# Self-attention softmax in a Trainium2 decoder layer: exp per head on ScalarE straight from the scores, causal mask on VectorE

## The reference

```python
q = (x @ wq).reshape(B, T, N_KV, N_REP, HEAD_DIM)
k = einsum('bkhl,ld->bkhd', (x @ wk_down).reshape(B, T, N_KV, D_LAT), wk_up)
v = einsum('bkhl,ld->bkhd', (x @ wv_down).reshape(B, T, N_KV, D_LAT), wv_up)
scores = einsum('bqhrd,bkhd->bhrqk', q, k) * HEAD_DIM ** -0.5
probs = softmax(where(causal, scores, min), axis=-1)
y = einsum('bhrqk,bkhd->bqhrd', probs, v).reshape(B, T, 1024) @ wo
...
x = x + self_attention(layernorm(x))
x = x + cross_attention_and_mlp(layernorm(x), ctx)
x = x + quantised_ffn(x)          # bitlinear, gelu, bitlinear
```

## Time and profile before

| | |
|---|---|
| median of 3 runs | 319.96 us (319.79 to 321.28) |
| the profiled execution, its own time | 321.1 us |
| its span, first to last instruction | 319.2 us |
| PE / PEld busy | 95% / 78% of the span |
| DVE busy | 86% |
| ACT busy | 60% |
| POOL busy | 51% |
| granted TensorE clock, mean | 0.984 of full |

### The profile page before, as it was taken

One profiled execution on the slowest core, in us unless ns is written; L12 is line 12 of the kernel. 1 busy time (PEld: TensorE's weight loads), 2 busy tenths in 40 slices (PEclk: granted clock), 3 DMA queues, 4 the chain that ended last, 5 costly groups with the idle time before them and its releaser, 6 DMA issues.

```text
span 319.2 us, 8883 instructions
## 1 busy us (share of the span) xinstructions
PE 302.6 (95%) x3185; PEld 248.8 (78%) x3198; DVE 273.2 (86%) x488; ACT 191.0 (60%) x369; POOL 161.5 (51%) x315
## 2 busy tenths in 40 slices
PE   8798999999999999999999999999999999998756
PEld 8476787879888887897788878887887888786534
DVE  2228996898989799999999999989999998999973
ACT  3164435436247759478966854497445965776852
POOL 7337006282933523671778266306660485077873
PEclk9899999999999999999999999999999999999978
DMA  7999000000000000000001010000000010000011
GB/s 200 340 368 330 6 3 0 2 2 0 4 2 2 3 0 2 3 0 2 2 3 34 3 35 2 2 0 4 16 18 2 2 37 2 0 3 33 3 34 66
DMA packets 11954, 12.54 MB, mean 39 GB/s; under 512 B 1668, under 2 KB 11144, under 8 KB 11912
## 3 DMA queue, kind: packets, MB, share of 16 engines
q1 hardware_dynamic: 10648, 11.40, 10.9%
q10 hardware_dynamic: 1264, 0.59, 0.7%
HBM read 9.89 MB, written 2.10 MB: 38 GB/s over the span
## 4 chain that ended last, share of the span: by engine, by line
PE 77%; issue 6%; DVE 6%; POOL 5%; ACT 5%; DVEq 0%; POOLq 0%; ACTq 0%
PE bank L1724 8%; PE bank L1871 7%; PE bank L1804 6%; PE bank L1894 6%; PE bank L1822 6%; PE bank L1903 5%; PE quad L1784 4%; PE bank L1885 4%; PE bank L1730 4%; PE quad L1861 3%; PE bank L1942 3%; PE bank L1757 3%; PE bank L1718 2%; PE bank L1923 2%; PE bank L1932 2%
## 5 line engine op out<-in xcount | busy, mean ns | idle before, releaser
L845 ACT ACTIVATE c_p<-bank 77x512 f32<-77x512 f32 x64 | 35.7, 591 | 26.4 <-PE bank L1871 26.2
L1871 PE MATMUL bank<-ident,c_s 128*77 128x128 f32 x256 | 34.8, 274 | 0.4 <-DVE f_o L1369 0.4
L564 POOL TENSOR_SCALAR f_s<-f_mv 128x1 f32<-128x1 f32 x16 | 3.5, 220 | 62.0 <-DVE f_s L1325 61.4
L821 ACT ACTIVATE a_p<-bank 128x512 f32<-128x512 f32 x48 | 27.3, 601 | 10.5 <-PE bank L1804 10.1
L1894 PE MATMUL bank<-c_y,xw_s 128*128 128x128 f32 x256 | 31.5, 276 | 0.8 <-DVE c_y L1303 0.8
L1871 PEld LDWEIGHTS bank<-ident,c_s 128*77 128x77 f32 x256 | 29.5, 148 | 3.1 <-issue 1.0
L1894 PEld LDWEIGHTS bank<-c_y,xw_s 128*128 128x128 f32 x256 | 30.1, 192 | 1.3 <-issue 0.9
L1903 PE MATMUL bank<-xw_s,c_h 128*128 128x256 f32 x128 | 30.5, 381 | 0.0
L1273 DVE TENSOR_REDUCE c_nm<-quad 128x16 f32<-128x1232 f32 x16 | 23.0, 1436 | 4.2 <-PE quad L1861 4.1
L1903 PEld LDWEIGHTS bank<-xw_s,c_h 128*128 128x128 f32 x128 | 23.3, 190 | 3.6 <-ACT c_h L854 0.5
L1284 DVE TENSOR_TENSOR c_s<-quad,c_nm 128x616 f32<-128x616 f32 x32 | 24.5, 792 | 1.3
(11 more groups left out here) (139 smaller groups left out, 769.8 us busy)
## 6 DMA issues: line engine op xcount, KB each, us to landing
out<-f_o SPq DMA_DIRECT2D x16, 128.0 KB, 1.7
xres<-in_x SPq DMA_DIRECT2D x1, 1536.0 KB, 10.0
c_p<-in_wqT SPq DMA_DIRECT2D x2, 512.0 KB, 6.9
c_p<-in_wo SPq DMA_DIRECT2D x1, 1024.0 KB, 9.6
f_h<-in_fw1T SPq DMA_DIRECT2D x1, 1024.0 KB, 12.1
c_s<-in_fw2T SPq DMA_DIRECT2D x1, 1024.0 KB, 11.3
xw_s<-in_xw SPq DMA_DIRECT2D x2, 512.0 KB, 9.7
fb_s<-in_fb SPq DMA_DIRECT2D x1, 512.0 KB, 6.3
```

The source lines that it names most:

```text
L821: nc.scalar.activation(dst, src, ACT.Exp, scale=SCALE_SA).then_inc(sa.sem["act"], 1)
L845: nc.scalar.activation(c_p[0:M, :, qt * P:(qt + 1) * P].rearrange("p (c j g) t -> p c j g t", c=KC, g=Q2)[:, :, j, :, :], bank("xs", f"tr{ ...
L1871: last = nc.tensor.transpose(dst[0:M, g * P:(g + 1) * P], c_s[:, qt, j, g, :], ident[:, :])
```

## The change

The causal mask leaves TensorE: `sa_mask`, a VectorE add, writes it into `quad` over the 128 x 128 diagonal block of all 8 heads at once. `sa_sub` is gone. ScalarE computes the exp from `quad` with the row maximum as bias, one instruction per head (8 for A of 128 columns, 8 for B of 256), each with an accumulated row sum in `a_sum`; `quad` is now released by the last of these. What is transposed are exps, so the step behind `sa_tr` is a plain copy, on ScalarE in all six cases. The sums no longer come out of `so_pv`: `sa_inv` on VectorE takes the reciprocal of the sums, each repeated 32 times (256 values per partition), for A and for B; TensorE transposes it (`so_rd`, 4 transposes), ScalarE copies the result to `a_rd`, and `so_y` is one multiply per half. The factor of the scores moves into the folded weights.

```diff
 def sa_exp(i, u, r):                                   # ScalarE
+    act.wait_ge(*sa.after("dve", f"mx{u}", i))
+    for c in range(KC):
+        nc.scalar.activation(s[:, r, c, :], quad[:, r, c * w:(c + 1) * w], ACT.Exp, bias=nm[:, r, c:c + 1],
+                             accum_out=a_sum[:, qt, c, r:r + 1]).then_inc(sa.sem["act"], 1)
+def sa_copy(i, u, n):                                  # ScalarE
+    dst, src = transposed_scores(i, u, n)
+    nc.scalar.activation(dst, src, ACT.Copy).then_inc(sa.sem["act"], 1)
-    nc.scalar.activation(dst, src, ACT.Exp, scale=SCALE_SA).then_inc(sa.sem["act"], 1)
+def so_rd(i):                                          # ScalarE
+    copied(so, "so", "rd", i, flat(a_rd))
+def sa_mask(i, u):                                     # VectorE
+    diagonal = quad[:, :, 0:KC * w].rearrange("p r (c m) -> p r c m", c=KC)[:, :, :, w - P:w]
+    nc.vector.tensor_tensor(diagonal, diagonal, mask2[:, 0:P].unsqueeze(1).unsqueeze(1).to_broadcast([P, 4, KC, P]), op=ALU.add)
-def sa_sub(i, u, e):                                   # VectorE, twice per unit
-    nc.vector.tensor_tensor(s[:, r, :, :], quad[...], nm[...].to_broadcast([P, 2, KC, w]), op=ALU.add)
+def sa_inv(i, u):                                      # VectorE
+    nc.vector.reciprocal(a_r[:, qt, :, :, :], a_sum[:, qt, :, :].unsqueeze(3).to_broadcast([P, KC, 4, L]))
 def so_y(i, c):                                        # VectorE
-    nc.vector.transpose(a_t[...], src[:, T:2 * T])
-    nc.vector.reciprocal(a_r[:, c, :], a_t[:, c, :, 0])
-    nc.vector.transpose(a_rd[...], a_r[:, c, :].unsqueeze(2).to_broadcast([P, NB, 32]))
     nc.vector.tensor_tensor(a_y[:, c, :], bank("so", f"pv{c}", i)[:, 0:T], a_rd[:, c, :], op=ALU.mult)
 def sa_scores(i, u):                                   # TensorE
-    for r in range(4):
-        last = mm(dst[r][:, 0:KC * P], identb[:, :], mask2[:, :], start=False, stop=True)
 def so_pv(i, c):                                       # TensorE
-    for off in (0, T):
     for t in range(TT):
         for r in range(4):
+def so_rd(i):                                          # TensorE
+    for c in range(KC):
+        for qt in range(TT):
+            last = nc.tensor.transpose(bank("so", "rd", i)[...], a_r[:, qt, c, :, :].rearrange("p r l -> p (r l)"), ident[:, :])
 QUAD_EMPTIED = {
-    ("sa", "suA"): ("dve", ("sbA0", "sbA1")),
+    ("sa", "suA"): ("act", ("exA01", "exA11", "exA21", "exA31")),
```

More of the change, by code:

```diff
@@ new lines, in _ @@
+            xs_exp(1, 1, 3)
+            xs_exp(1, 1, 1)
+            sp_q(4)
+            xs_exp(1, 1, 0)
+            sa_exp(3, "B", 3)
+            sa_exp(3, "B", 2)
+            xp_xT(2)
+            sa_exp(3, "B", 0)
+            xs_exp(1, 1, 2)
+            sa_exp(3, "B", 1)
+            xp_q(2)
+            sa_copy(3, "A", 0)
+            xs_exp(1, 0, 0)
+            sa_copy(3, "B", 2)
+            sp_v(4)
+            sp_xT(5)
+            so_rd(3)
+            sa_copy(3, "B", 0)
+            f1_qT(0, 0)
@@ new lines, in _ @@
+            f1_gelu(1, 0)
+            sa_copy(5, "A", 1)
+            f2_ssq(1, 0)
+            xp_q(3)
+            f2_hT(0, 1)
+            sp_k(6)
+            xp_xT(4)
+            f1_gelu(1, 1)
+            sa_copy(5, "B", 3)
+            sa_copy(5, "B", 0)
+            f1_pre(4)
+            f2_pre(4)
+            xs_exp(3, 0, 3)
+            xs_exp(3, 0, 0)
+            xs_exp(3, 0, 2)
+            xs_exp(3, 0, 1)
+            f2_ssq(1, 1)
+            xp_q(4)
+            sa_copy(5, "A", 0)
@@ new lines, in _ @@
+            f1_qT(2, 0)
+            f2_hT(1, 0)
+            xs_exp(3, 1, 0)
+            xs_exp(3, 1, 2)
+            f1_qT(2, 1)
+            sa_copy(5, "B", 1)
+            f2_pre(5)
+            xm_relu(3, 0)
+            xs_exp(3, 1, 1)
+            xs_exp(3, 1, 3)
+            f2_pre(6)
+            sa_copy(5, "B", 2)
+            f1_pre(5)
+            f1_pre(6)
+            f1_gelu(2, 0)
+            f2_hT(1, 1)
+            sp_xT(7)
+            so_rd(5)
+            f2_ssq(2, 0)
+            sp_v(6)
@@ L1228, in sa_sub @@
             @element
[L1229 to L1236 removed]
+            def sa_inv(i, u):
+                qt = 0 if u == "A" else 1
+                for r in range(4):
+                    dve.wait_ge(*sa.after("act", f"ex{u}{r}1", i))
+                dve.wait_ge(*so.after("pe", "rd", i - 1))
+                nc.vector.reciprocal(a_r[:, qt, :, :, :], a_sum[:, qt, :, :].unsqueeze(3).to_broadcast([P, KC, 4, L])).then_inc(sa.sem["dve"], 1)
@@ new lines, in _ @@
+            f2_hT(3, 1)
+            xm_w1(5, 1)
+            f1_l1(4, 2)
+            xs_tr(6, 1, 3)
+            xo_pv(6, 0)
+            f2_l2(3, 0)
+            xp_xT(7)
+            xm_w2(5, 1)
+            f1_qT(5, 0)
+            xs_tr(6, 1, 2)
+            xp_q(7)
+            f1_l1(5, 1)
+            xs_tr(6, 1, 0)
+            f2_hT(4, 0)
+            xs_scores(7, 0)
+            xs_tr(6, 1, 1)
+            xm_w1(6, 0)
+            f1_qT(5, 1)
+            f1_l1(5, 0)
+            xo_pv(6, 1)
```

1878 lines of the change are left out of this document (947 added, 931 removed).

## The result

The changed kernel takes 329.27 us (median of 4 runs, 328.12 to 331.38) against 320.62 us for the kernel before in the same job (319.79 to 321.34): a ratio of 1.028, 95% interval 1.021 to 1.034. It is slower by 2.8%; the prediction was 316.8 us in a range of 307 to 326. The profiled execution took 331.38 us with a span of 329.5 us; before, these were 321.1 and 319.2. The profiled execution of the changed kernel is the slowest of its four, so the two traces lie 10.3 us apart where the medians differ by 8.7.

The account below looks back on a forecast made before the run. The prediction took TensorE and VectorE to be full side by side in the middle. Head -2.4, VectorE's work -2.0, score waits -2.5, hand-over +2.7 and ScalarE late +1.0 made -3.2: 319.96 to 316.8 us, range 307 to 326.

Parts of the forecast that it names:

- the head: Start of the kernel: first mask and maximum move ahead of VectorE's 7.48 us wait for x; -2.4 us.
- VectorE's own work: VectorE over the whole kernel: 47.0 us removed, masks 19.4 and reciprocals 25.6 added; net -2.0 us.
- the bound of 1.77: Upper price in us of one 256-value reciprocal on VectorE, at 6.3 ns per value; VectorE's net then +0.7 us.
- TensorE: TensorE over 8 batches: passes over `ones` and mask matmuls removed (17.6 us), transposes added (3.5 us); net -14.1 us.
- quad eased: VectorE's 5.0 us of waits for scores in `quad`: a lighter TensorE gives back half, -2.5 us.
- hand-over: `quad` held through exps and next scores; one uncovered place, batch 2 unit B to batch 3 unit A: +2.7 us.
- ScalarE +1.0: ScalarE still inside another instruction when maxima land: 0.26 us at about four places without cover, +1.0 us.
- 191 to 242 us: ScalarE's busy time before and after, not the bound; exps start 0.35 us apart in unit A, 0.45 in B.
- Rival 2: ScalarE's exps and accumulator reads do not overlap and hold `quad` 1.7 us longer per unit; 327 us, chance 0.17.
- Rival 1: 256-value reciprocal costs 438 ns, TensorE becomes the bound: -14.1, +3.5 for shorter hand-over covers; 309.4 us, chance 0.2.
- The tail: End of the kernel: a chain of feed-forward steps that keep their durations, so no change.
- Slower: Over 321.6 us, chance 0.24: forecast's spread 0.02, ScalarE as the last wait 0.17, eight-cycle reciprocal 0.05.

Follow-up runs that it names:

- e12_head: Changed kernel with short reciprocals (8 sums inverted, then copied) and three context projections put back to the start of TensorE's order; 312.51 us, ratio 0.977.
- e8_before_more: Kernel before plus one unused VectorE maximum over 1024 scores ahead of each of the 16 maxima; 334.49 us, ratio 1.038.
- the table of four: Middle of four kernels: mask on TensorE or VectorE, reciprocals short or long; TensorE idle 3.7, 4.5, 8.5 and 12.9 us.
- e11_no_sums: Changed kernel without the accumulated row sums (sums a constant 1, rows not divided); 329.81 us, ratio 1.031.
- e3_small_inv: Changed kernel with the reciprocal over 8 sums and a copy over 32 rows, in place of the reciprocal over 256 values; 314.93 us, ratio 0.980.
- e1_warm: Changed kernel with 18 throw-away warm-up matmuls at the start in place of 12; 328.70 us, ratio 1.022.
- e2_fill: e1_warm plus six throw-away matmuls ahead of the first transposes of the reciprocals; against the changed kernel's 329.27 us, 328.22 us, ratio 1.023.
- e4_both: Changed kernel with both edits of e2_fill and the short reciprocals of e3_small_inv; 316.42 us, ratio 0.985.

## Why the prediction was wrong

- **The sign came from the head.** "So 2 x 1.2 = 2.4 us of VectorE's work move into idle time" is the step that failed. I priced the head's first 22 us and took the rest of it for unchanged. The start is indeed earlier, but by 1.1 us at the first maximum (21.6 instead of 22.6) and by 0.7 at `wsum`, since TensorE stood idle where three projections had been and its clock was at 0.50 from 8 to 18 us. Behind `wsum` the changed kernel then loses 10.6 us, so the term was +9.9 and not -2.4. What I left out there: the reciprocals of batch 0 stand directly ahead of TensorE's transposes and on a busy VectorE (6.4 us with the clock that falls behind them), and the new order itself is 4.2 us longer there. A chain through a first batch has little of other batches' work beside it.
- **VectorE's own work**, -2.0: measured +0.4 in all (273.2 to 273.6), because the reciprocal took 1.74 us and not 1.6. The price was right to 9% and the bound of 1.77 nearly met. The Trainium skill's repeat count of 8 for the reciprocal (VectorE: DVE Perf Modes, Walkthrough: the 8-slice pipeline in each mode), read as eight cycles per value, gave 2.3 us as an estimate. The trace doesn't agree: from 8 to 256 values it is (1736 - 184) / 248 = 6.3 ns per value.
- **TensorE**, -14.1: measured -13.4 us of work between the residuals of batch 0 and 7, and -13.7 over the whole span in `e12_head` (302.6 to 288.9), whose mean clock is near that of before (0.989 against 0.984). Right.
- **The middle as a whole** (own work -2.0, quad eased -2.5, hand-over +2.7, ScalarE +1.0: -0.8): measured -1.9. Right in sign and within 1.1 us. That two engines are full side by side fits `e8_before_more` and the table of four. The waits of VectorE bear the single terms out, though no run prices them. Its 5.0 us for scores at L1273 and L1225 became 1.9 at L1385. The hand-over that I placed near 75 us is there, at 85.7: the maxima of unit B of batch 2 start at 78.81 us and take 2.29, the mask on batch 3 starts 4.6 us after their end (forecast 4.6), and VectorE is idle for 2.46 of it (forecast 2.7). From 60 to 260 us the mask waits twice:

```profile
DVE quad L1329 <- PE quad L1895: 2.6, 2, 2.5
```

- **ScalarE** (191 to 242 us, 0.35 and 0.45 us apart): right. Rival 2 named two signs. Waits of VectorE for scores of over 10 us did come: 9.5 us for the mask and 1.9 for cross-attention's maxima, against 5.8 of the same kinds before. But 5.3 of them lie in the head, TensorE waited for the exps before it wrote scores for only 2.1 us in the whole span, and the exps start 0.342 and 0.448 us apart, so the overlap that rival 2 needed to be lost is there. `e11_no_sums`, which takes some 0.7 us per unit off ScalarE, shortened the middle by 1.7 us and moved the median not at all. So its mechanism did not set the time, though its 327 us come nearest to the result: near the right number for another reason.
- **Rival 1** (the reciprocal cheap): its mechanism is what `e3_small_inv` builds, the pair at 0.48 us instead of 0.44. Its -14.1 + 3.5 = -10.6 us stand beside -10.8 measured in the middle (210.7 to 199.9). Its whole span is only 5.8 us shorter than before (319.2 to 313.4), since head and tail give back 5.0, for which rival 1 had no term.
- **The tail**, nothing: the rest behind batch 7's residual was 2.3 us longer (63.7 to 66.0) and stayed at 65.9 to 67.8 in all kernels with the changed order, against 63.7 in both with the old one. The order leaves VectorE 1.9 us more to do there (53.34 to 55.27 us busy); that this is the cause is likely and not shown. I had priced the steps, not which of them are left at the end.
- **Slower** had 0.24, and none of its cases was a slow head. The range ended at 326; the median lies 3.3 us outside.

## What to carry to other kernels

Where two engines are full side by side, a change pays by what it does to the pair: the same edit (the mask moved from TensorE to VectorE) was worth 7 us with 18 us less on VectorE and nothing without that room. Price an elementwise operation by the values it writes before it is made to do a broadcast as well: eight values inverted and then copied cost 0.48 us, 256 inverted 1.74 us. And read the first batch apart from the steady state, with its own order of steps and with TensorE's clock, since little runs beside it that could hide a microsecond.

## What was not expected of the hardware

- The reciprocal's price goes by the values written: 8 values 184 ns, 56 values 444, 128 values 950, 184 values 1296, 256 values 1736. Over the 184 ns of 8 values that is 5.4 to 6.4 ns for each further value, where an add of 1024 values took 1224 ns.
- Adding in place in PSUM, both read and written there, took 1224 ns for 1024 values, within 1% of the add from PSUM to SBUF (1214).
- The same six additional throw-away matmuls at the start kept the clock at 1.00 up to 40 us in the profiled executions of `e1_warm` and `e2_fill` and not in that of `e4_both`, where it was 0.50 from 12 to 18 us; the three other executions of `e4_both` have a higher mean clock (0.989 to 0.995) than this one (0.983). So the clock differs between executions of one kernel, and what decides it was not found. Matmuls of the same form took 0.60 us at the full clock and 1.06 at half.
